# A turned expert loop, unchecked register reads and earlier tables in a one-core vision tower

## The reference, cut to what matters

```python
x = hidden_states.reshape(-1, h)                       # 832 tokens, 256 wide
shared_out = _swiglu(x, shared_gate_w, shared_up_w, shared_down_w)
logits = x @ gate_w                                    # 32 experts
topk_ids = jnp.argmax(logits, axis=-1)                 # one expert for a token
scores = jax.nn.sigmoid(jnp.max(logits, axis=-1))[:, None]
xs = x * scores
sorted_x = xs[jnp.argsort(topk_ids)]                   # tokens by expert
g = ragged_dot(sorted_x, routed_gate_w, tokens_per_expert)
u = ragged_dot(sorted_x, routed_up_w, tokens_per_expert)
d = ragged_dot(silu(g) * u, routed_down_w, tokens_per_expert)
return shared_out + d[inverse order]                   # and the residual is added
```

## Time and profile before

| | before |
|---|---|
| median of 3 runs | 354.65 us |
| the profiled execution | 352.22 us |
| its span, first to last instruction | 350.4 us |
| mean granted TensorE clock in it | 0.951 |
| busy: TensorE, VectorE, ScalarE, GpSimd | 86%, 59%, 38%, 16% of the span |
| moved | 67.73 MB, mean 193 GB/s |

### The profile page before, as it was taken

The page is one execution under the profiler, slowest core; times in us unless marked ns, Lnnn a source line. Parts: engine busy times, 40 slices in busy tenths (PEclk is TensorE's granted clock), DMA queues, the critical chain, the costliest instruction groups (busy, mean ns, idle before and its releaser), DMA issues.

```text
span 350.4 us, 6874 instructions
## 1 busy us (share of the span) xinstructions
PE 300.3 (86%) x2484; PEld 213.8 (61%) x2484; DVE 206.3 (59%) x589; ACT 134.8 (38%) x309; POOL 56.0 (16%) x73
## 2 busy tenths in 40 slices
PE   1996979388899999999975999989899999964958
PEld 1774548277899999998963766665454555421322
DVE  0454684433465665665266699948739867645653
ACT  1021242243242242242233466529147545615650
POOL 0111000100110110110000001111711210442350
PEclk9999899879999999999997799999999999996996
DMA  7999991003364264053597200000389996899231
GB/s 291 397 435 426 410 316 48 2 0 111 131 241 151 91 239 147 34 181 129 233 353 285 85 2 2 6 4 0 86 299 395 394 354 251 336 358 397 49 46 17
DMA packets 13115, 67.73 MB, mean 193 GB/s; under 512 B 1738, under 2 KB 7322, under 8 KB 8986
## 3 DMA queue, kind: packets, MB, share of 16 engines
q1 hardware_dynamic: 11050, 64.28, 47.9%
q0 software_dynamic: 2032, 3.02, 4.1%
HBM read 61.38 MB, written 5.91 MB: 192 GB/s over the span
## 4 chain that ended last, share of the span: by engine, by line
PE 64%; issue 11%; DMA 10%; DVE 8%; ACT 3%; SPq 1%; DVEq 1%; POOL 1%; ACTq 0%
PE P L340 17%; PE P L460 8%; PE P L448 8%; PE P L628 7%; DMA arena<-experts_dram 7%; PE P L374 4%; PE P L484 4%; PE P L510 3%; PE P L436 2%; PE P L641 2%; DMA vrow<-sorted_x 2%; DMA arena<-patches_dram 2%; PE P L525 1%; DVE arena L996 1%; PE P L535 1%
## 5 line engine op out<-in xcount | busy, mean ns | idle before, releaser
L340 PE MATMUL P<-arena 128*104 128x256 f32 x288 | 73.5, 395 | 9.4 <-DMA arena<-patches_dram 7.1
L340 PEld LDWEIGHTS P<-arena 128*104 128x104 f32 x288 | 47.4, 176 | 22.4 <-issue 8.3
L1290 POOL TENSOR_TENSOR rstd<-var,mhalf 104x1 f32<-104x1 f32 x40 | 21.9, 548 | 210.5 <-DVE var L919 210.5
L628 PE MATMUL P<-arena,cols 128*32 128x512 f32 x288 | 37.3, 664 | 11.1 <-ACT cols L849 9.1
L824 ACT ACTIVATE arena<-arena 128x1024 f32 x31 | 31.5, 1051 | 21.2 <-SPq L325 9.1
L460 PE MATMUL P<-arena 128*128 128x104 f32 x256 | 29.9, 275 | 2.4 <-ACT arena L764 2.4
L460 PEld LDWEIGHTS P<-arena 128*128 128x128 f32 x256 | 29.7, 192 | 3.1 <-issue 1.4
L448 PEld LDWEIGHTS P<-arena 128*128 128x128 f32 x256 | 29.8, 192 | 1.2 <-issue 0.7
L448 PE MATMUL P<-arena 128*128 128x104 f32 x256 | 29.8, 275 | 0.5 <-issue 0.5
L628 PEld LDWEIGHTS P<-arena,cols 128*32 128x32 f32 x288 | 9.1, 120 | 32.6 <-issue 19.1
L764 ACT ACTIVATE arena<-P,arena 128x104 f32<-128x104 f32 x64 | 17.0, 348 | 27.7 <-PE P L448 27.7
(11 more groups left out here) (200 smaller groups left out, 480.3 us busy)
## 6 DMA issues: line engine op xcount, KB each, us to landing
arena<-experts_dram SPq DMA_DIRECT2D x22, 1536.0 KB, 8.4
arena<-experts_dram SPq DMA_DIRECT2D x8, 2048.0 KB, 12.7
arena<-patches_dram SPq DMA_DIRECT2D x4, 624.0 KB, 6.3
sorted_x<-arena SPq DMA_DIRECT2D x1, 2056.0 KB, 35.2
arena<-shared_dram SPq DMA_DIRECT2D x1, 1536.0 KB, 32.4
arena<-w_dram SPq DMA_DIRECT2D x1, 1024.0 KB, 9.8
out_dram<-arena SPq DMA_DIRECT2D x1, 1024.0 KB, 33.7
out_dram<-h POOLq DMA_DIRECT2D x8, 104.0 KB, 4.9
```

Source lines behind the costliest of these rows:

```text
L340: last = mm(P[b][0:a.shape[1], col:col + D], a, rhs(c), start=(c == 0), stop=(c == chunks - 1))
L628: last = mm(P[b][part, :], xT[:, c, part], weights(u)[:, c * INNER:(c + 1) * INNER], start=(c == 0), stop=(c == DC - 1), tile_position=(0, ...
L1290: nc.gpsimd.tensor_tensor(rstd[:, :], var[:, :], mhalf[:, :], ALU.pow).then_inc(s["rstd_ready"], 1)
```

## The change

- **Turned loop.** Turns 0 to 6 are written out. A turn of the loop fetches rows, does gate and up of quad 7 + i (counted from 0), then the down product of the quad before it. The last down product, its output copy and its addition come behind the loop. The loop's down weights always use the even buffers (LAST = 0). DVE waits for the loop's last addition to land before it writes the last output. ACT and DVE read a turn's registers at its start.
- **Unchecked reads.** `weights_of` and `entry` read their registers without a check on each; one check of a value is left in either (the count of feeds, and `free`).
- **Lanes free with the table.** `x3T` moves to `qT`, `zB` to the front of `quad`; the lanes no longer overlap what the shared products read, and DVE copies the first quad's weights among `hidden(5)` to `hidden(7)`, ACT no longer waits for the last `hidden`.
- **Tables sooner.** The feed transposes follow `shared_up(3)` instead of `shared_up(4)`, the strip transposes `shared_up(4)` instead of `shared_up(5)`; `hidden(3)` moves behind the feed table's copy. SyncE issues the second feed before it waits for the scatters and the first window.
- **Outputs in fetched rows.** `y_evac` writes to the row tile `xw` of its own quad, and no longer waits for additions. `yw` is gone.
- **Shared down products** are placed by a tuple, SHARED_AT.

```diff
+SHARED_FIRST = 1
+SHARED_AT = ((1,), (2, 3), (4, 5), (6, 7), (), (), ())
+LAST = (STILL - 1) % 2
-        oT = x3T = kz
+        oT = kz
+        x3T = qT
-        zB = flat5[:, 0:2 * HALF].rearrange("p (a n) -> p a n", a=2)
+        zB = quad[:, 0:2 * HALF].rearrange("p (a n) -> p a n", a=2)
...
-            _, found = nc.values_load_multi_w_load_instructions(row, engines=[engine.engine], min_val=0, max_val=(SLOTS - 1) * SLOT)
-            return found[LANES], found[0:LANES]
+            _, found = nc.values_load_multi_w_load_instructions(row, engines=[engine.engine], min_val=0, max_val=(SLOTS - 1) * SLOT,
+                                                                skip_runtime_bounds_check_because=IN_TABLE)
+            return nc.s_assert_within(found[LANES], 1, EXPERTS + 1), found[0:LANES]
...
             feed(entry(0), 0)
             second = entry(1)
+            feed(second, 1)
             sp.wait_ge(xs_sent, 16 * GROUPS)
-            window(0)
-            feed(second, 1)
-            for i in range(1, len(WINDOW_PARTS)):
+            for i in range(len(WINDOW_PARTS)):
                 window(i)
...
-            for n in range(2, 5):
+            for n in range(2, 4):
                 shared_up(n)
             pe.wait_ge(s["feeds_ready"], 1)
...
-            shared_up(5)
+            shared_up(4)
             pe.wait_ge(s["blocks_ready"], 1)
...
TensorE behind the turns:
+            pe.wait_ge(s["xT_ready"], STILL)
+            pe.wait_ge(s["y_ready"], STILL - 1)
+            pe.wait_ge(s["l_added"], 16)
             with pe.Fori(0, more) as i:
-                pe.wait_ge(s["l_hT_ready"], i + 1)
-                for n in ("copied_dve", "copied_act"):
-                    pe.wait_ge(s[n], i + (STILL + 2))
-                pe.wait_ge(s["l_y_ready"], i + 1)
-                down_strips(STILL % 2).then_inc(s["l_dn_done"], 1)
-                pe.wait_ge(l_window_in, 16 * (i + 2))
+                pe.wait_ge(l_window_in, 16 * (i + 1))
                 xt(STILL).then_inc(s["l_xt_done"], 1)
                 pe.wait_ge(s["l_xT_ready"], i + 1)
                 pe.wait_ge(s["l_gatew_in"], 2 * (i + 1))
                 strips(0, gate_of).then_inc(s["l_gate_done"], 1)
+                pe.wait_ge(s["l_upw_in"], 2 * (i + 1))
                 strips(2, up_of).then_inc(s["l_up_done"], 1)
+                pe.wait_ge(s["l_hT_ready"], i + 1)
+                for n in ("copied_dve", "copied_act"):
+                    pe.wait_ge(s[n], i + (STILL + 1))
+                pe.wait_ge(s["l_y_ready"], i + 1)
+                down_strips(LAST).then_inc(s["l_dn_done"], 1)
                 pe.wait_ge(s["l_hw_ready"], i + 1)
                 ht().then_inc(s["l_ht_done"], 1)
+            pe.wait_ge(s["hT_ready"], STILL)
+            for n in ("copied_dve", "copied_act"):
+                pe.wait_ge(s[n], more + (STILL + 1))
+            pe.wait_ge(s["l_y_ready"], more + 1)
+            down_strips(LAST).then_inc(s["dn_done"], 1)
...
ScalarE's loop, as it is after:
+            act.wait_ge(s["up1_done"], STILL)
             with act.Fori(0, more) as i:
+                need, where = weights_of(act, i + STILL)
+                act.wait_ge(s["loaded"], need)
+                copy_third(where[2], 0, gate_of(2))
+                copy_third(where[3], 0, gate_of(3)).then_inc(s["l_gatew_in"], 1)
                 act.wait_ge(s["l_ht_done"], i + 1)
                 hT_evac().then_inc(s["l_hT_ready"], 1)
+                act.wait_ge(s["l_xt_done"], i + 1)
                 xT_evac().then_inc(s["l_xT_ready"], 1)
+                copy_third(where[2], 1, up_of(2)).then_inc(s["l_upw_in"], 1)
                 act.wait_ge(s["l_gate_done"], i + 1)
                 silu_gate().then_inc(s["l_sgate_ready"], 1)
+                act.wait_ge(s["l_dn_done"], i + 1)
+                copy_third(where[2], 2, down_of(2, LAST)).then_inc(s["copied_act"], 1)
+            act.wait_ge(s["l_ht_done"], more + 1)
+            hT_evac().then_inc(s["hT_ready"], 1)
...
VectorE, end of the loop and behind it:
                 mul().then_inc(s["l_hw_ready"], 1)
+                dve.wait_ge(s["l_dn_done"], i + 1)
+                y_evac(xw[:, STILL - 1, 0:D]).then_inc(s["l_y_ready"], 1)
+                copy_down(where, LAST).then_inc(s["copied_dve"], 1)
+            dve.wait_ge(s["l_added"], 16 * (more + 1))
+            dve.wait_ge(s["dn_done"], STILL)
+            y_evac(y_last).then_inc(s["y_ready"], 1)
...
GpSimd:
             with pool.Fori(0, more) as i:
-                pool.wait_ge(s["l_aim_ready"], i + 1)
-                pool.wait_ge(s["l_xt_done"], i + 1)
                 pool.wait_ge(s["l_turn"], i + 1)
-                window(i + (STILL + 1))
+                pool.wait_ge(s["l_prev_ready"], i + 1)
                 pool.wait_ge(s["l_y_ready"], i + 2)
...
-                add_rows(STILL, s["l_added"])
+                add_rows(STILL - 1, s["l_added"])
+                pool.wait_ge(s["l_xt_done"], i + 1)
+                pool.wait_ge(s["l_aim_ready"], i + 2)
+                window(i + (STILL + 1))
+            pool.wait_ge(s["y_ready"], STILL)
+            add_rows(STILL, added)
```

129 lines of the change are left out of this document (56 added, 73 removed).

## The result

The changed kernel takes 358.28 us in the median of 20 runs, where the kernel before takes 353.68 beside it: a ratio of 1.0147 with a 95% interval of [1.0114, 1.018], so 1.5% slower. The prediction was 352.9, 0.5% under the 354.65 us known then, with a range up to 357.0: wrong in sign and outside the range.

The account below looks back on a forecast made before the run. Gapless TensorE quads carry the first quad's start through; the removed tail gives the gain. Last landing 347.7 plus 0.9 late start made 348.6 against 350.4, -1.8 us; with the profile-to-median difference 352.9 us, range 351.4 to 357.0.

Parts of the forecast that it names:

- the tail: From quad 8's gate product at 331.8 us, through products at full clock, to the last addition's landing at 347.7.
- The start: First quad: scatters land between 256 and 260.7, the window at 263.65 behind two feeds, so it starts 0.9 us late.
- The room of the removal: At the program's end: from the last addition's landing at 344.3 to the span's end at 350.4, at most 6.1 us gain.
- rival B: At quad 8: TensorE's clock falls in the turn's idle stretch, +1.7 to +2.9 us, centre 355.4 us; chance 0.25.
- Quad 8's start: In the loop: ACT waits for a down product, then reads registers and copies; gate at 331.8, 2.8 us later than before.
- rival C: At the start: scatters crawl under the feeds, landing at 262.9, window at 268.6; 357.9 us, slower; chance 0.14.
- The two additions at the end: Behind quad 8: quad 7's addition lands at U + 7.7, the last is issued at U + 8.5 and lands at U + 12.3.
- U: The end of quad 8's gate and up products at full clock, forecast at 335.4 us.
- the cover: While DVE waits for quad 7's landing: weight copies, evacuation and last down product cost nothing; beyond 1.7 us more they would show.
- Quads 1 to 6, lanes, shared products: Middle of the kernel: sooner lane copies, SHARED_AT and the feeds from the tenth change the time by 0.
- Checks: Register reads: each check costs 0.28 us, taken from five registers read on DVE.
- From the profile to the median: Sum to median: the earlier median, 354.65, lay 2.4 us above the profiled 352.22, so that difference was applied.

Follow-up runs that it names:

- Before again: The kernel before, run a second time with nothing changed, for a second profile: 353.59 us, ratio 1.0028.
- after again: The changed kernel, run a second time with nothing changed, for a second profile: 358.94 us, ratio 1.0154.
- front half alone: The kernel before with only the change's tables, feeds, lanes and unchecked reads, keeping the old loop and outputs: 354.61 us, ratio 1.0053.
- windows first: The changed kernel with SyncE waiting for the scatters and loading the three windows before the first two feeds: 359.78 us, ratio 1.0219.
- reads ahead: The changed kernel with ScalarE's read and copies for quad 8 and VectorE's register read ahead of the wait for quad 6's down product: 356.62 us, ratio 1.0089.

## Why the prediction was wrong, step by step

The step that failed is the tail, from quad 8's gate product to the end of the span. The forecast had 15.9 us there (331.8 to 347.7), before had 21.4, after has 20.8: of the 5.5 us that the removed quad was to give back, 0.6 came. Two terms that the sum had at nothing fill it, GpSimd's drain and the clock. The start and quad 8's delay, the losses that the forecast did count, came out near their sizes.

- **The room of the removal, a term left out.** I took 344.3 to 350.4 us, 6.1 us, as what the ninth quad stood in front of, and left "1.8 around its span" alone. But GpSimd drains its queue for 2.27 us behind its last addition, in before hidden under the ninth quad (344.5 to 346.8), in after at the very end. The room was at most 350.4 - 346.8 = 3.6 us. The term missed, from the last landing to the span's end, is 352.7 - 349.9 = 2.8 us. No run takes the drain away; that it is on the path is read from the rows, in which it ends 0.2 to 0.3 us ahead of the span's end in every kernel with the turned loop, and 2 us or more ahead of it in those with the old one.
- **The clock, rival B, was right** and should have been the forecast: quad 8's products 6.35 us instead of 3.64 at a mean clock of 0.56, +2.7, near the upper end of B. My rows had 1.0 us without a fall and 3.65 us with one, and the gap of 3.4 that came is next to the second. I gave the clock 0.25 although my own working put the gap at 3.0 us.
- **Quad 8's start.** Forecast 2.8 us later than before; counted from quad 7's gate it is 3.4 us in the first profiles and 3.0 in the second. The mechanism held (ScalarE waits for a down product, then reads). The runs split it in part: ScalarE's wait and VectorE's read, moved together, give 1.3 us (12.0 to 10.7 in the table), and ScalarE's read behind its next wait 1.0 of idle time (1.63 to 0.67 us). The rest is not split.
- **The start.** I placed the scatters' landing between 256 and 260.7 and the window with the second feed at 263.65. They landed at 260.97, past my upper end and towards rival C, but the window no longer had a feed in front, and the first quad came at 264.04. On the clock of the page that is 0.2 us late, counted from the feed table's last column 0.5 in the first profile and 1.35 in the second: 0.9 lay between them. SyncE's part had a wrong reason: the 3.4 us from the table's copy to the first feed were not mostly three checked reads. Before again took 2.1 us for the same stretch, and after with the checks back 1.96; what the other 1.3 us of the first profile were is open. The forecast had 2.05 us there (249.45 to 251.5), 1.4 less than before; two checks less give 0.6 of them, and no run shows the term for the other 0.8. After took 1.44 us (249.06 to 250.50).
- **The two additions at the end.** Last addition at U + 8.5 forecast, U + 7.8 measured (338.26, 346.06), landing 3.8 as taken. The last down product ended at 344.35, 1.0 us ahead of the last output copy, so the cover that I had priced at 1.7 us held. The landing of quad 7's addition took 4.0 us and not 4.7.
- **Quads 1 to 6, lanes, shared products.** Forecast 0; the middle stage differs by 0.1 us between the second profiles.
- **Checks.** Forecast 0.28 us each, measured 0.23 to 0.26 in the kernel with checks.
- **From the profile to the median.** Span terms: forecast 348.6, found 352.7; drain +2.8, clock +2.7, start -0.7, and -0.7 in the tail. I then moved the sum by the 2.4 us that lay between profile and median before. For after 358.28 - 354.4 = 3.9 us lie there, for before 353.68 - 352.22 = 1.5. That third part of the miss is the spread of executions, which a single pair of profiles can't show: ahead of the feed table's last column after again is 4.4 us longer than the first profile, and before again 3.0 us. The program is the same there. From 66 to 82 us the granted clock was 0.79 in both first profiles and 0.68 in both second ones. Why it varies was not settled.

## What to carry to other kernels

Before taking the last useful landing as the end of a shorter kernel, look what each engine still has to do behind it, its end drains included (2.28 us on GpSimd here); work that is removed may have been their cover. When a reorder opens a gap ahead of matmuls, price the matmuls at the lower clock unless your own rows show a gap of that length that left it up (behind 3.4 us quad 8's took 6.35 us here instead of 3.64). Filling the gap with idle products gave back 3.8 us here where the fill fitted, and nothing where it overran the gap or where the next transfer was the bound, so close the gap first. When a copy moves ahead of a wait, list what it passes on its own engine and who waits for that.

## What the runs showed of the hardware

- The last indirect scatter issued while two 1.5 MB weight feeds start landed 8.3 to 8.8 us after issue (after, after again, front half alone); with no feed beside them scatters landed in 2.7 us in the median (windows first).
- The drain behind an indirect addition on GpSimd takes 2.27 to 2.28 us, in both kernels and every profile.
- Idle time alone does not say what TensorE's clock does. Ahead of quads 7 and 8 the granted clock was 1.00 over products behind 0.67, 0.83, 0.96 and 1.09 us of idle time (3.94 us behind the first, 3.64 behind the others). Behind each gap of 3.3 us or more they took 4.94 to 6.54 us at a mean of 0.55 to 0.73, even behind one that followed 7 us of idle products (5.34 us, 0.68). Of gaps near 1.6 us, those behind idle products (1.45, 1.64, 1.69) and the one behind a quad 7 at full clock (1.70, the kernel before with idle products) left it up (3.64 us, 1.00); those behind a quad 7 that had itself run slow (1.63 and twice 1.68) did not (5.33 and 5.34 us, 0.67). A short piece of work in a long gap did not help either: with 3.19 us of idle time, two transposes and 0.56 us more, quad 8 took 4.90 us (0.74).
- The clock can fall after the gap, inside the products: with reads ahead it was 1.00 up to 335.3 us, where they start, and 0.50 from 337 to 339 (5.34 us, a mean of 0.67).
- From the end of ScalarE's wait to its first weight copy, with a register read of five values in between, lay 1.7 us in after and with reads ahead; with the read made ahead of the wait, 0.3 us, and there the weights' landing was the releaser.
